# Fourier transform of the image rows: even frequencies from folded quarter rows, a new order of its first pieces, and the weight loads at other places

## The reference, cut to what matters

```python
Vf   = jnp.fft.rfft(phi, n=n, axis=0)             # 16 filters
Uf_p = jnp.fft.rfft(u, n=n, axis=1)               # u: the normed tokens of each image
Uf_m = jnp.fft.rfft(u * sgn3, n=n, axis=1)
U_plus  = jnp.fft.irfft(Vf[None, :, :, None] * Uf_p[:, :, None, :], n=n, axis=1)[:, :sl]
U_minus = jnp.fft.irfft(Vf[None, :, :, None] * Uf_m[:, :, None, :], n=n, axis=1)[:, :sl] * sgn
out = einsum('btkd,k,kde->bte', U_plus, s, Mpp) + einsum('btkd,k,kde->bte', U_minus, s, Mpm)
out = out + (three taps of u through M_u)         # added to the residual
```

## Time and profile before

| | us |
|---|---|
| median of 3 runs | 2060.93 (2059.23 to 2061.85) |
| profiled execution, its own time | 2059.56 |
| span of its profile | 2058.2 |
| TensorE busy in the span | 1941.7 (94%) |
| DVE, ACT, POOL busy | 1163.5, 1093.9, 612.3 |
| mean granted TensorE clock, share of full | 0.976 |

### The profile page before, as it was taken

The page is one execution under the profiler, slowest core; times in us unless marked ns, Lnnn a source line. Parts: engine busy times, 40 slices in busy tenths (PEclk is TensorE's granted clock), DMA queues, the critical chain, the costliest instruction groups (busy, mean ns, idle before and its releaser), DMA issues.

```text
span 2058.2 us, 64954 instructions
## 1 busy us (share of the span) xinstructions
PE 1941.7 (94%) x27483; PEld 1397.2 (68%) x27483; DVE 1163.5 (57%) x3209; ACT 1093.9 (53%) x2122; POOL 612.3 (30%) x780
## 2 busy tenths in 40 slices
PE   4899999989999888999999999999999999989998
PEld 2566666666666665665677777777777777767776
DVE  2567778878767653240465665665655656633332
ACT  4678887778766552222555555555555555500000
POOL 5344455555545430120422121222222121100000
PEclk8799999999999889999999999999999999999999
DMA  4332323323323223469322212221222112486651
GB/s 98 92 86 73 98 76 85 102 79 97 96 81 84 67 80 82 121 161 203 108 60 51 55 35 60 60 60 47 54 60 51 45 45 59 118 206 178 161 147 48
DMA packets 281600, 183.63 MB, mean 89 GB/s; under 512 B 55416, under 2 KB 279360, under 8 KB 279520
## 3 DMA queue, kind: packets, MB, share of 16 engines
q1 hardware_dynamic: 278942, 178.99, 33.5%
q10 hardware_dynamic: 2304, 0.40, 0.2%
q0 software_dynamic: 64, 0.08, 0.0%
HBM read 108.87 MB, written 70.63 MB: 87 GB/s over the span
## 4 chain that ended last, share of the span: by engine, by line
PE 75%; DVE 9%; issue 4%; POOL 4%; DMA 4%; ACT 3%; SPq 2%; DVEq 0%; POOLq 0%; ACTq 0%
PE banks L1279 19%; PE banks L1262 19%; PE banks L1444 10%; PE banks L1121 7%; PE banks L384 5%; PE banks L378 3%; DVE zone L583 2%; PE banks L343 2%; PE banks L333 2%; PE banks L357 2%; DVE st L570 1%; DMA W<-Un 1%; PE banks L391 1%; PE banks L431 1%; DVE W L623 1%
## 5 line engine op out<-in xcount | busy, mean ns | idle before, releaser
L1312 DVE COPY Gm<-banks 128x896 f32<-128x896 f32 x448 | 488.2, 1091 | 348.8 <-PE banks L1262 348.8
L1298 ACT ACTIVATE Gm<-banks 128x896 f32<-128x896 f32 x448 | 412.1, 920 | 318.7 <-PE banks L1262 314.1
L1262 PE MATMUL banks<-V,zone 118*128 118x224 bf16 x3584 | 438.1, 261 | 1.9 <-ACT qT L1133 0.6
L1279 PE MATMUL banks<-Gm,U 128*32 128x128 f32 x12544 | 434.9, 276 | 3.7 <-POOL U L1339 1.8
L1262 PEld LDWEIGHTS banks<-V,zone 118*128 118x128 bf16 x3584 | 291.9, 98 | 125.1 <-issue 44.8
L1279 PEld LDWEIGHTS banks<-Gm,U 128*32 128x32 f32 x12544 | 316.3, 110 | 85.2 <-issue 83.1
L1327 POOL COPY U<-UL 128x896 f32<-128x896 f32 x28 | 50.5, 1803 | 636.1 <-PE banks L1279 504.1
L1444 PE MATMUL banks<-YC,zone 98*98 98x256 f32 x1024 | 227.8, 381 | 1.3 <-DVE YC L1501 1.3
L1444 PEld LDWEIGHTS banks<-YC,zone 98*98 98x98 f32 x1024 | 169.8, 166 | 54.5 <-DVE YC L1501 1.8
L840 POOL TENSOR_TENSOR W<-W,mx 128x280 f32<-128x280 f32 x196 | 130.4, 666 | 229.6 <-DVE mx L630 229.5
L1121 PE MATMUL banks<-XR,W 98*128 98x392 f32 x512 | 175.5, 500 | 4.7 <-DVE W L1146 4.2
(11 more groups left out here) (142 smaller groups left out, 2275.7 us busy)
## 6 DMA issues: line engine op xcount, KB each, us to landing
Yd<-YS SPq DMA_DIRECT2D x112, 224.0 KB, 4.3
W<-Vd SPq DMA_DIRECT2D x392, 49.0 KB
UL<-Ud SPq DMA_DIRECT2D x28, 448.0 KB, 4.3
zone<-Yd SPq DMA_DIRECT2D x32, 392.0 KB
YL<-Yd SPq DMA_DIRECT2D x32, 392.0 KB
zone<-Mbf SPq DMA_DIRECT2D x28, 256.0 KB
Vd<-W SPq DMA_DIRECT2D x112, 56.0 KB
T<-XR SPq DMA_DIRECT2D x28, 224.0 KB, 3.2
```

Of the source, the lines that this page charges most:

```text
L1262: ins = e.matmul(pt[:, q, :], self.M[:, par, 64 * half + 4 * i + q, :], self.V[P % 2][:, par, :], start=True, stop=True)
L1279: ins = e.matmul(p[32 * x:32 * x + 32, :], self.U7[(2 * P + ch) % 3][:, sl, 8 * (3 - q):8 * (3 - q) + 32], self.Gm[:, par, r:r + 2, :], st ...
L1298: e.activation(dst, src, ACT.Copy).then_inc(S["gm_act"], 1)
L1312: v.tensor_copy(dst, src).then_inc(S["gm_dve"], 1)
```

## The change

Four things are changed.

1. The even frequencies are taken over folded vectors. A new step `f_fold` lets DVE make four sums and differences of the halves of `EV` and `OD` (98 partitions x 512 each). An even piece is then two groups of two fp32 products of 196 columns, where it was four of 392. Odd pieces stay as they were. The second turn of a half image now reverses rows of `UA` and not of `UR`. The tables have 4704 columns per partition instead of 6272.
2. Half image 0 is turned in unit f + 1 instead of f + 4; two of its odd pieces come first, (0, 6) in f + 3 and (0, 7) at the end of f + 4; its other pieces follow from f + 5 on. Each later piece lies one unit earlier than before, and turn (w, 0) comes before piece (w - 1, 6) instead of behind it. The exchange matrix and f_load 0 are issued ahead of the tables.
3. w_load 0 stays in f + 29. w_load 1 goes behind f_store 4 in f + 30, still ahead of f_load 7 in f + 31; w_load 2 stays behind f_store 5 (now in f + 33).
4. w_load 3 goes into the filters' list of loads, behind the second load of rows of `Ud`.

SP's order in the stretch that matters is then: f_load 6, w_load 0, f_store 4, w_load 1, f_load 7, f_store 5, w_load 2, f_store 6, u_load, f_store 7.

```diff
     f = LEAD + NT * 4 + 7
+    put(f - 1, rests="f_rev")
+    put(f - 1, rests="f_load", n=0)
     put(f - 1, rests="f_tables")
-    for w in range(2):
-        put(f - 1, rests="f_load", n=w)
+    put(f - 1, rests="f_load", n=1)
     for at, (w, i) in enumerate(SPECTRUM_ORDER):
-        u = f + 4 + at // 2 if at < 60 else f + 34 + (at - 60) // 4
+        u = f + 1 if at < 2 else f + 3 + at // 2 if at < 60 else f + 33 + (at - 60) // 4
         if i < 2:
             put(u, rests="f_turn", n=2 * w + i)
-            if i == 1 and w + 2 < 6:
-                put(u, rests="f_load", n=w + 2)
+            if i == 1:
+                put(u if w else u + 2, rests="f_fold", n=w)
+                if w + 2 < 6:
+                    put(u, rests="f_load", n=w + 2)
+        elif at == 2:
+            put(f + 3, rests="f_dft", n=8 * w + i - 2)
+        elif at == 3:
+            put(f + 4, fills="f_dft", n=8 * w + i - 2)
         else:
             put(u, rests="f_dft", n=8 * w + i - 2)
         if w % 2 and i in (5, 9):
             put(u, rests="f_store", n=w - 1 + (i == 9))
-        if w == 5 and i == 9:
-            put(u, rests="w_load", n=2)
-            put(u + 1, rests="w_load", n=3)
+        if (w, i) in ((5, 5), (5, 9)):
+            put(u, rests="w_load", n=i // 4)
...
     put(f + 29, rests="w_load", n=0)
-    put(f + 30, rests="w_load", n=1)
     put(f + 31, rests="f_load", n=7)
...
+SPECTRUM_PIECES = [(6, 7, 2, 3, 0, 4, 5, 1, 8, 9) if w == 0 else (2, 3, 4, 5, 0, 6, 1, 7, 8, 9) for w in range(2 * NB)]
...
 class Spectrum:
     def tensor(self, e, k, n):
...
-            for a in range(4):
-                ins = e.matmul(p[:, 0:392], src[:, a, 128 * m:128 * m + 128], self.F[:, c, a, 392 * half:392 * half + 392],
-                               start=a == 0, stop=a == 3)
+            if blk == 0:
+                for h in range(2):
+                    for a in range(2):
+                        ins = e.matmul(p[:, 196 * h:196 * h + 196], self.fold[:, c, h, a, ms], self.Fev[:, c, h, a, :],
+                                       start=a == 0, stop=a == 1)
+            else:
+                src = (self.EV, self.OD)[c][w % 2]
+                for a in range(4):
+                    ins = e.matmul(p[:, 0:392], src[:, a, ms], self.Fodd[:, c, a, :], start=a == 0, stop=a == 3)
...
     def vector(self, v, k, n):
+        elif k == "f_fold":
+            w, ev, od = n, self.EV[n % 2], self.OD[n % 2]
+            v.wait_ge(S["evod"], 2 * w + 2)
+            if w:
+                v.wait_ge(S["dft"], SPECTRUM_DONE[w - 1, 5])
+            v.tensor_tensor(self.fold[:, 0, 0], ev[:, 0:2, :], ev[:, 2:4, :], ALU.add)
+            v.tensor_tensor(self.fold[:, 0, 1], ev[:, 0:2, :], ev[:, 2:4, :], ALU.subtract)
+            v.tensor_tensor(self.fold[:, 1, 0], od[:, 0:2, :], od[:, 2:4, :], ALU.subtract)
+            v.tensor_tensor(self.fold[:, 1, 1], od[:, 0:2, :], od[:, 2:4, :], ALU.add).then_inc(S["folded"], 1)
...
     def sync(self, e, k, n):
+        if k == "f_rev":
...
+            e.wait_ge(S["pv"], NB * NT)
+            e.dma_start(self.rev[:, :], D["c_rev"]).then_inc(S["d_u0"], 16)
+        elif k == "f_tables":
             e.dma_start(self.F, D["c_fwd"]).then_inc(S["d_fwd"], 16)
...
 class Filters:
...
                 if c:
                     load_rows(e, D, S, c)
+                if c == 1:
+                    load_weights(e, D, S, 3)
```

More of the change, by code:

```diff
@@ L864, in gpsimd @@
                     q.dma_start(self.D["VbD"][par, 112:118], self.D["c_ar"][par]).then_inc(S["d_ar"], 16)
[L868 to L881, removed]
     def load_x(self, e, b, J0, J1):
@@ L1059, with load_weights @@
 """).split()
-SPECTRUM_ORDER = [(0, 0), (0, 1)] + [(w + (i < 2), i) for w in range(2 * NB) for i in (2, 3, 4, 5, 6, 0, 1, 7, 8, 9)
+SPECTRUM_PIECES = [(6, 7, 2, 3, 0, 4, 5, 1, 8, 9) if w == 0 else (2, 3, 4, 5, 0, 6, 1, 7, 8, 9) for w in range(2 * NB)]
+SPECTRUM_ORDER = [(0, 0), (0, 1)] + [(w + (i < 2), i) for w in range(2 * NB) for i in SPECTRUM_PIECES[w]
                                      if w + (i < 2) < 2 * NB]
 SPECTRUM_USE = {piece: i for i, piece in enumerate(SPECTRUM_ORDER)}
+SPECTRUM_DONE = {(w, i): 8 * w + 1 + [j for j in SPECTRUM_PIECES[w] if j >= 2].index(i) for w in range(2 * NB) for i in range(2, 10)}
+def load_weights(e, D, S, n):
+    M = D["zone"][:, :].bitcast(BF16).rearrange("p (a x) -> p a x", a=2)
+    if n == 0:
+        e.wait_ge(S["xnu"], 2 * ROWS)
+        for i in range(3):
+            e.wait_ge(S[f"d_mo{i}"], 32 * 9)
+    par, cs = n % 2, slice(8192 * (n // 2), 8192 * (n // 2) + 8192)
+    for k, (m, _) in enumerate(TERMS):
+        e.dma_start(M[16 * k:16 * k + 16, par, cs], D["Mbf"][par, m][:, cs]).then_inc(S[f"d_m{n}"], 16)
+    for r, tap in ((112, par), (115, 2)):
+        e.dma_start(M[r:r + 3, par, cs], D["MUd"][:, tap, cs]).then_inc(S[f"d_m{n}"], 16)
 class Spectrum:
@@ L1616, in tables @@
     NP_, J = 1568, 784
-    even = np.arange(0, 784, 2)
+    even = np.concatenate([np.arange(0, 784, 4), np.arange(2, 784, 4)])
     odd = np.arange(1, 784, 2)
     slots = np.concatenate([even, odd])
-    j = np.arange(392)[:, None] + 0.5
+    near = np.arange(196)[:, None] + 0.5
+    rows = np.concatenate([near, 392 - near])
     th = lambda a, f: 2 * np.pi * a * f / NP_
-    fe, fo = even[None, :].astype(float), odd[None, :].astype(float)
-    fi = fe.copy()
-    fi[0, 0] = 784.0
-    Fe = np.concatenate([np.cos(th(j, fe)), -np.sin(th(j, fo))], 1)
-    Fo = np.concatenate([np.cos(th(j, fo)), -np.sin(th(j, fi))], 1)
-    fwd = np.stack([Fe, Fo], 0).reshape(2, 4, 98, 784).transpose(2, 0, 1, 3)
+    fo = odd[None, :].astype(float)
+    fi = even[None, :].astype(float)
+    fodd = np.stack([-np.sin(th(rows, fo)), np.cos(th(rows, fo))]).reshape(2, 4, 98, 392).transpose(2, 0, 1, 3)
+    fev = np.empty((2, 2, 2, 98, 196))
+    for h in range(2):
+        f = fi[:, 196 * h:196 * h + 196]
+        top = f.copy()
+        if h == 0:
+            top[0, 0] = 784.0
+        fev[0, h] = np.cos(th(near, f)).reshape(2, 98, 196)
+        fev[1, h] = -np.sin(th(near, top)).reshape(2, 98, 196)
+    fwd = np.concatenate([fodd.reshape(98, 3136), fev.transpose(3, 0, 1, 2, 4).reshape(98, 1568)], 1)
     jj = np.arange(784)[:, None].astype(float)
```

46 lines of the change are left out of this document (27 added, 19 removed).

## The result

| | before | after |
|---|---|---|
| median, us | 2061.39 (4 runs) | 2039.43 (4 runs, 2036.55 to 2042.47) |
| ratio to before | | 0.9893 [0.9871, 0.9915] |
| profiled execution, its span | 2058.2 | 2040.6 |
| TensorE busy | 1941.7 | 1904.5 |

The kernel is 22 us faster. The forecast was 2032 with a range of 2016 to 2041, so sign and range held, and the gain came 7 us short of the 29 that were forecast.

A forecast was written before the change was run, and what follows sets the result against it. TensorE's own work was taken as the bound. 42 + 6 + 3.7 us come off it, but 28.9 arrive past the wait for f_load 7: 2059.56 - 28.9 = 2030.7, median 1.4 higher, 2032; main case 2024 to 2040, stated range 2016 to 2041.

The forecast's parts named there:

- Even pieces: Spectrum on TensorE: an even piece costs 1.32 us instead of 2.63, so 32 pieces give up 42 us.
- Folds: DVE in the spectrum: four fold instructions per half image at 0.6 us each, with 0.4 and 1.0 as ends.
- They are hidden: Folds from w = 1 on fit beside turns on DVE, 7.9 us ahead of their first user; only w = 0 could show.
- Start: Start of the spectrum: two odd pieces done by 787.9, gaining 6.0 us, plus 3.7 us of clock.
- f_load 6: SP's queue: f_store 3 at 868.7, 31.6 us earlier, then 16 us to this load at about 885, 30 us earlier.
- that sign: SP's queue: the prediction is wrong if f_load 6 is issued after 890.
- the two stated reasons: Between f_store 3 and f_load 6: SP issues twiddles for 5.96 us, and DVE waits 6.31 for a store to land.
- f_load 6 to f_load 7: From the first's issue to the second's landing stays 45.1 us, landing at 930; TensorE stands still for 21 us.
- The side sum of the weights: DMA engines before f_load 7: two w_loads are 3.9 MB, taking 28 us at 131 GB/s.
- From there to f_store 6: From f_load 7's landing: 22.7 us including 3.7 of half clock, f_store 6 issued at 952.7, 28.9 us earlier.
- w_load 3 ... costs nothing: Filters: the load in its new place has at least 21 us for 14 before filter stage 3.
- Behind it nothing changes: After f_store 6: POOL's reshaping, the same four odd pieces and the first filters stay as before, so 28.9 us arrive.

The follow-up runs named there:

- even_full: The changed kernel with even pieces back at four products of 392 columns, from the folded vectors and odd table; results wrong; 2067.18 us, ratio 1.0017.
- late_start: The changed kernel with half image 0 turned in unit f + 4 and all pieces in their old units; 2048.32 us, ratio 0.9922.
- the control: The changed kernel run once more, unedited, for the other runs to be compared with; 2041.7 us, ratio 0.9884.
- g_late: The changed kernel with g_load (spectra and twiddles) issued behind w_load 0 instead of in unit f + 24; 2046.53 us, ratio 0.9928.
- best_c: The changed kernel with wider weight loads, f_load 7 directly behind f_load 6, w_load 2 and 3 behind the filters' second and third row loads; 2022.01 us, ratio 0.9797.
- f7_first: The changed kernel with f_load 7 issued directly behind f_load 6, ahead of w_load 0; 2029.26 us, ratio 0.9816.
- w_wide: The changed kernel with each w_load as fewer, wider DMAs (48, 32, 16 and 16 partitions instead of seven times 16), same bytes; 2034.9 us, ratio 0.9851.
- no_w3: The changed kernel with w_load 3 left out and a constant in its place, so results are wrong; 2034.11 us, ratio 0.985.
- w3_back: The changed kernel with w_load 3 back behind w_load 2, ahead of f_store 6, as in the kernel before; 2042.44 us, ratio 0.9886.
- w_wide_f7: The changed kernel with wider weight loads and f_load 7 directly behind f_load 6; 2027.17 us, ratio 0.9816.
- best_a: The changed kernel with the edits of w_wide_f7 and g_late, and w_load 2 behind w_load 1; 2027.52 us, ratio 0.9833.
- best_b: best_a with w_load 3 cut into two halves, behind the second and third load of rows; 2028.15 us, ratio 0.9834.

## Why the prediction was right, and where it was 7 us off

**Even pieces: right.** 1.33 us a piece (1.32 expected), so the weight load of 0.19 doesn't bound. Their instructions are busy for 44.6 us in after and 86.5 in even_full: the 42. TensorE's whole busy time falls by 37.2 only (1941.7 to 1904.5), because odd pieces and turns now take 5.7 us more, at the half clock behind the stops.

**Folds: 0.6 us each, right (but for one of 1.0 at w = 4 and one of 1.7 at w = 0), but not free everywhere.** "They are hidden" held but for half image 4, whose first even piece waits 0.60 us for its fold. And it left out what is queued behind them on DVE. First that wait of PE, then DVE after (columns as in rows 4):

```profile
873.34 5.57 PE L1141 MATMUL banks<-XR 98*128 98x196 f32 x32 [0.60 <-DVE XR L1184]
...
870.41 1.07 DVE L1181 TENSOR_TENSOR XR<-W 98x512 f32<-98x512 f32 x1
...
872.60 0.68 DVE L1184 TENSOR_TENSOR XR<-W 98x512 f32<-98x512 f32 x1
873.20 0.67 DVE L690 TENSOR_TENSOR XR<-XR,banks 112x512 f32<-112x512 f32 x1
```

The addition L690 of the linear attention waits behind the fold of half image 4, its store to T (873.90) stands ahead of f_store 3 in SP's queue, and f_store 3 comes at 872.2 in the places of before, where 868.7 was forecast. ACT had its piece out of the bank at 869.0, so the pieces were on time and SP's queue was not.

**Start: right.** Two odd pieces were done at 787.6 in the places of before (787.9 forecast), the clock was full, and late_start gives 8 us for the 9.7.

**f_load 6: 889.5 for 884.7 (the 885).** 3.5 us of it are the step above, and the rest is 17.4 us instead of 16 from f_store 3 on. The prediction called itself wrong if f_load 6 came after 890. Without the shift it came at 893.28 and in the control at 890.33, so that sign is missed only because the shift is taken off. The twiddles, the first of the two stated reasons, fell in g_late; the second, DVE's rows waiting for a store to land and SP for the rows, is what stays.

**The stop at half image 5: missed.** The row was there: DVE waits for a store's landing before it writes the last normed rows. Now turn (5, 1) stands right behind that wait on DVE, and TensorE behind the turn: 4.40 us, and a half clock after it. It seems to have cost nothing at the end, since f_load 7 was later still (no run takes it away), and stays in best_c (4.29), as the largest stop there before the filters.

**f_load 6 to f_load 7: right.** 45.1 forecast, 39.9 and 44.2 measured. The stop is 12.3 and 16.5 where 21 was forecast, because TensorE itself came later (in after at 917.2 for 909; 6.7 of these 8 us are the stop at half image 5 and its half clock). That the weights in front are the cause is shown by f7_first, which takes them away, and by w_wide, which makes them shorter. The side sum of the weights is off: 2 x (7 x 256 + 2 x 48) KB at 131 GB/s are 29.5 us and not 28; little hangs on it, since the 45.1 was read whole. The chances given add up to 1.02.

**From there to f_store 6: right.** 22.7 forecast, 21.7 measured (933.20 to 954.90), half clock included. f_store 6 is then 30.4 us earlier than before, where 28.9 was forecast. To here the sum held.

**The step that failed: "w_load 3 ... costs nothing".** I asked only whether it lands in time for filter stage 3, and it does; no stage waited for zone. I didn't ask what 14 us of full DMA engines do to the rest of the stage, nor did I have TensorE's own instructions among the transfers. "Behind it nothing changes" was wrong: from f_store 6 to the first store to `Yd` it was 50.3 us before and is 58.0 after. By no_w3 w_load 3 costs 7 to 8 us: what the second row load feeds is 1.8 later, then the hole of 3.3 to 4.8, then the half clock. 30.4 less 7.6 is 22.8 at that store, and the medians say 22. In the kernel before w_load 3 lay in a stretch where nothing waited for it; w3_back shows that this place was gone as well once TensorE had become faster.

## What to carry to other kernels

When an engine gets faster, list the transfers that it used to cover and put each one's time from issue to landing beside the new distance. Here the order of the SP queue, and not TensorE, decided how much of 42 us arrived, and a new order of four of its loads, with the weights' loads made wider, gave another 15 to 18 us (best_c). A transfer that lands in time can still cost: it stands in the rings ahead of others (f_store 5 took 22.49 us to land behind weights), it holds the issuing queue (14.83 us in g_late), and it delays an engine's own instructions (the hole). A stop without a releaser is worth a look at the instruction queue on the profile's page. Where a load can be written as fewer DMAs to more partitions, it is worth a try: it was 2 to 4 us a load here.

## What was not expected of the hardware

- SP's issue of a DMA took longer when the engines were full: two twiddle loads took 2.8 us in the control (at 878.69) and 14.83 behind w_load 0.
- TensorE gets its instructions by the same 16 DMA engines, a packet of 16 KB for every 256 of them, and can run out of them while these are full. It stood for 2.5 to 5.5 us in the first stage of the filters in nine profiles (after, control, f7_first, w_wide, w_wide_f7, late_start, even_full, g_late, best_c), always with a packet of q8 that began 506 to 550 instructions after its forerunner and landed 1.5 to 2.1 us before TensorE went on. In before, no_w3, w3_back, best_a and best_b, where it began after 225 to 324, there is no such stop.
- The same 3.9 MB in DMAs of 48, 32 and 16 partitions took 4 to 8 us less than in DMAs of 16.
- One of the four folds of half image 0 took 1.75 us where the other three took 0.68 (L1183, at 789.14). Its cause was not tried.
